# An attention and feed-forward kernel: queries on a second queue, rotation quarters between maxima, and small weights loaded in the fourth group

## The reference

```
q, k, v = xn @ wq.T, xn @ wk.T, xn @ wv.T        # 16 heads of 64
q, k = rope(q), rope(k)                          # x1*c - x2*s, x1*s + x2*c
scores = (q @ k.T) * 64**-0.5, causal
out = softmax(scores) @ v
x = x + layernorm(out @ wo.T)
x = x + layernorm(ffn(layernorm(x)))             # swiglu, mixture of 8 experts, swiglu
```

## Time and profile before

| | |
|---|---|
| median of 3 runs | 1265.85 us (1264.65 to 1266.01) |
| the profiled execution | 1265.46 us, its span 1263.7 us |
| PE busy | 1144.5 us, 91% of the span |
| DVE, ACT, POOL busy | 980.8, 958.8, 946.8 us |
| mean granted TensorE clock | 0.97 of full speed |
| first scores | at 62.09 us |

### The profile page before, as it was taken

The page is one execution under the profiler, slowest core; times in us unless marked ns, Lnnn a source line. Parts: engine busy times, 40 slices in busy tenths (PEclk is TensorE's granted clock), DMA queues, the critical chain, the costliest instruction groups (busy, mean ns, idle before and its releaser), DMA issues. The chain is left out here.

```text
span 1263.7 us, 34875 instructions
## 1 busy us (share of the span) xinstructions
PE 1144.5 (91%) x13531; PEld 789.1 (62%) x13531; DVE 980.8 (78%) x2230; ACT 958.8 (76%) x2199; POOL 946.8 (75%) x984
## 2 busy tenths in 40 slices
PE   4689999999989999999999999999999588999995
PEld 1246667676766676766767676767677355666562
DVE  7799777787968787878878787978575559767987
ACT  3668888878787878788787879787889665756574
POOL 3568889889898889898988889898767465334462
PEclk8699999999999999999999999999999798999996
DMA  6652425244251515252524425151601100000011
GB/s 200 146 134 65 115 59 134 61 109 102 67 135 35 135 35 136 56 124 59 135 63 108 106 63 131 39 135 35 152 19 47 51 1 2 1 1 2 1 34 34
DMA packets 50660, 97.03 MB, mean 77 GB/s; under 512 B 6720, under 2 KB 23360, under 8 KB 48448
## 3 DMA queue, kind: packets, MB, share of 16 engines
q1 hardware_dynamic: 50496, 94.81, 30.0%
HBM read 58.47 MB, written 34.60 MB: 74 GB/s over the span
## 5 line engine op out<-in xcount | busy, mean ns | idle before, releaser
L795 POOL TENSOR_TENSOR Plo<-P,Phi 128x512 f16<-128x512 f32 (+3 forms) x640 | 538.7, 868 | 128.5 <-ACT P L486 127.9
L483 ACT ACTIVATE Phi<-psS 128x512 f16<-128x512 f32 (+3 forms) x768 | 383.7, 500 | 148.9 <-PE psS L341 105.1
L486 ACT ACTIVATE P<-psS 128x512 f32<-128x512 f32 (+3 forms) x640 | 306.3, 479 | 0.0
L335 PE MATMUL psS<-Q,K 128*128 128x512 f16 (+3 forms) x768 | 251.5, 327 | 41.1 <-DVE Plo L642 37.1
L362 PE MATMUL psO<-V,Plo 128*128 128x65 f16 x2304 | 288.3, 194 | 0.0
L358 PE MATMUL psO<-V,Phi 128*128 128x65 f16 x2304 | 287.0, 192 | 0.0
L360 PE MATMUL psO<-V,Phi 128*128 128x64 f16 x2304 | 286.1, 191 | 0.0
L691 DVE TENSOR_REDUCE pmax<-psX 128x1 f32<-128x512 f32 x384 | 252.4, 683 | 23.6 <-PE psX L422 15.0
L358 PEld LDWEIGHTS psO<-V,Phi 128*128 128x128 f16 x2304 | 219.5, 98 | 56.6 <-issue 0.3
L338 PE MATMUL psS<-Q,K 65*128 65x512 f16 (+3 forms) x768 | 251.7, 328 | 0.0
L422 PE MATMUL psX<-K,Q 128*128 128x512 f16 (+4 forms) x768 | 226.5, 330 | 12.0 <-DMA Q<-HL 3.1
(11 more groups left out here) (197 smaller groups left out, 2165.0 us busy)
## 6 DMA issues: line engine op xcount, KB each, us to landing
K<-k_way SPq DMA_DIRECT2D x48, 512.0 KB, 7.1
k_way<-HL SPq DMA_DIRECT2D x64, 256.0 KB, 3.9
q_way<-HL SPq DMA_DIRECT2D x60, 256.0 KB, 3.8
Q<-q_way SPq DMA_DIRECT2D x60, 256.0 KB, 6.9
Q<-q_way SPq DMA_DIRECT2D x15, 512.0 KB, 11.7
out<-y SPq DMA_DIRECT2D x8, 256.0 KB, 2.2
y<-in_x SPq DMA_DIRECT2D x3, 512.0 KB, 10.9
hn<-in_x SPq DMA_DIRECT2D x3, 512.0 KB, 5.7
```

What stands on the lines that cost most here:

```text
L335: nc.tensor.matmul(out, M.K1[:, p, h, j * P:(j + 1) * P], M.Q1[:, p, h, c:c + w], start=True, stop=False)
L483: nc.scalar.activation(M.Phi[:, U % NP_, 0:w], X, ACT.Exp, scale=SCALE)
L486: nc.scalar.activation(full, X, ACT.Exp, scale=SCALE).then_inc(S.exp_done, 1)
L795: nc.gpsimd.tensor_tensor(M.Plo[:, U % NP_, 0:w], M.P32[:, U % NP_, 0:w], M.Phi[:, U % NP_, 0:w], ALU.subtract).then_inc(S.lo_pool, 1)
```

## The change

Five edits:
- `weights_later`: the thirteen small weight transfers move from SP's queue in the opening to the fourth group (slot 3), between the sending of its queries and the wait for its row of maxima.
- `first_query`: the four Q1 transfers of heads 0 and 1 are issued from ACT's queue, right behind the fourth rotated quarter's cast; those of heads 2 and 3 stay on SP's.
- First keys: each head's keys are loaded by a transfer of its own, as soon as that head's have arrived in DRAM, and TensorE waits head by head.
- The order of side items in slot -1: the second key quarter, both query quarters and the first two V pairs stand later, between and behind maxima; `X_SQUARE` places the batches of squares one by one.
- In the joins of maxima the copy is written as a maximum over one element.

```diff
-QK_EARLY = ((2, 3, 4, 5, 6, 7, 8, 9), (0, 1, 2, 3, 16, 17, 18, 19))
-V_FIRST = ((-1, 4), (-1, 5), (0, 1), (0, 3))
+QK_EARLY = ((2, 3, 4, 5, 6, 7, 8, 9), (0, 1, 16, 17, 25, 26, 29, 30))
+V_FIRST = ((-1, 24), (-1, 27), (0, 1), (0, 3))
...
-X_SQUARE = {(-1, 5): (1, 2), (-1, 17): (3,)}
+X_SQUARE = {(-1, 5): (1,), (-1, 17): (2,), (-1, 18): (3,)}
...
+W_SLOT = 3
...
+    def first_query(eng, queue, h):
+
+        rows = slice(h * HALF, (h + 1) * HALF)
+        for k in range(2):
+            queue.dma_start(M.Q1[k * HALF:(k + 1) * HALF, 0, h, :], M.HL[rows, 1, k, :]).then_inc(S.first_q[h], 16)
...
-                    if k == 0 and h % 2 == 0:
+                    if k == 0 and (s < 0 or h % 2 == 0):
                         if s < 0:
-                            pe.wait_ge(S.first_k, 32)
-                            pe.wait_ge(S.first_q[h // 2], 16 * GH)
+                            pe.wait_ge(S.first_k[h], 16)
+                            pe.wait_ge(S.first_q[h], 32)
...
                     rope_hi(item)
+                    if (s, *item[2:4]) == (-2, 1, 1):
+                        act.wait_ge(S.rope_hi, 4)
+                        for h in range(2):
+                            first_query(act, nc.scalar, h)
...
-                nc.vector.tensor_copy(M.pmax[:, 1, h, 0:5:4], M.pmix[:, h, 0:2, 3]).then_inc(S.max_parts, 1)
+                nc.vector.tensor_reduce(M.pmax[:, 1, h, 0:5:4], M.pmix[:, h, 0:2, 3:4], AX.X, ALU.max).then_inc(S.max_parts, 1)
...
-                                 M.HL[h * HALF:(h + 1) * HALF, 0, :, :]).then_inc(S.first_out, 16)
-                sp.wait_ge(S.first_out, 16 * GH)
-                for i in range(2):
-                    sp.dma_start(M.K1[:, 0, 2 * i:2 * i + 2], krows[:, 2 * i:2 * i + 2]).then_inc(S.first_k, 16)
+                                 M.HL[h * HALF:(h + 1) * HALF, 0, :, :]).then_inc(S.first_out[h], 16)
+                for h in range(GH):
+                    sp.wait_ge(S.first_out[h], 16)
+                    sp.dma_start(M.K1[:, 0, h], krows[:, h]).then_inc(S.first_k[h], 16)
...
-            for k, name in enumerate(("lin0_w", "swi1_w1", "swi1_w2", "lin1_w", "swi2_w1", "swi2_w2")):
-                sp.dma_start(M.wd[:, k, :], I[name]).then_inc(S.w_in, 16)
...
+                if s == W_SLOT:
+                    weights_later()
                 taken(sp, (s, "mt"))
```

## The result

The changed kernel takes 1280.62 us (median of 4 runs, 1280.06 to 1280.89) where the one before takes 1265.93 (4 runs, 1264.65 to 1266.33): ratio 1.0116 [1.0103, 1.0128], slower by 14.7 us. Its profiled span is 1278.9 us, 15.2 over the span before. The sign and both losses were as forecast; the size was not: it lies 1.6 us above the end of the range, and one step of the mechanism, the early landing of the queries, did not happen.

The account below looks back on a forecast made before the run. TensorE was taken as the bound in steady groups. Opening +4.3, fourth-group wait +3.6, lower clock +1.5 and later copies -0.5 made +8.9 us, 1274.7 on the median 1265.85, stated as 1274.5; range 1267 to 1279.

Parts of the forecast that it names:

- Queries and keys sooner: Opening: queries issued from ACT land early, so the first maximum starts at 36.5, 5.5 us sooner (bounds 35.6 to 39.8).
- T': Start of the opening's first maximum in the changed kernel, forecast at 36.5 us, bounds 35.6 and 39.8.
- Rival C: Opening: queries still land behind the keys, only 0.9 us of earlier issue is won; first maximum 41.1, total 1279; 6%.
- T: Start of the opening's first maximum in the kernel before, 42.01 us, after 3.09 us of waiting for a query transfer.
- V2: Third V pair on DVE in the opening, forecast at 72.0 instead of 66.29 us: +5.8.
- the opening's sum: Opening: +5.8 us at the third V pair less 1.5 for the long copy, +4.3 (bounds +3.4 to +7.6).
- the fourth group's two terms: Moved weights delay the row of maxima: TensorE waits 3.6 us (2.8 to 4.3), its lowered clock costs 1.5 (0 to 1.7).
- the chain from T': Opening: squares, V casts and query rotations following the first maximum put the first exponential at T'+33.2 = 69.7, 6.3 us later.
- V0: First V pair in the opening: ACT's cast stands behind all squares, done T'+18.3; DVE, there at T'+13.2, stands still 5.1 us.
- r6: First of two query rotation quarters of the second group, on DVE; forecast to end at T'+22.5, formerly T+10.8.
- POOL's chain behind r6: Opening: sums, casts, L816 and the table load up to the first exponential, 10.7 us in all, which nothing shortens.
- From there both orders are the same: Opening, behind the third V pair: old and new order run alike, so its +5.8 us shift passes on.

## Why the prediction was right and wrong

**What failed: "Queries and keys sooner".** I put T' at 36.5, "near the quick end, as only 128 KB of its own queue stand there". Measured: 41.23. The queries landed in 7.2 us at the least, slower than the 6.9 I had as the worst. Giving them another queue removed the keys of the same queue from ahead of them and nothing else; the 1.5 MB still shared the transfer engines. Rival C had this, at T' = 41.1 and 1279, and I gave it 6%. The Trainium skill ("DMA: Bandwidth & Descriptors", "Issuing engines are not separate DMA queues") says that all issuers share the same 16 engines; the traces agree: not more than the issue time was gained, T' is 0.8 us before T. The trace of before had spoken too: a later query transfer, issued when the keys had landed, took 2.7 us, those behind the keys 5.1 to 6.9. I read the difference as a place in a queue, without a row that said so. Holding back the bytes and not the queue brought 2.0 to 2.7 us. This one step is worth 4.7 us at T' and, with the roundings of the chain behind it, 4.9 at V2 (76.96 for 72.0); the opening's sum with it, +4.3 + 4.9, is the measured +9.2. With T' alone put right the forecast would have been 1279.2; the rest is the fourth group's two terms, below.

**What held: the chain from T'.** Measured against T', with the prediction in brackets: DVE's stop 5.10 us (5.1), V0 at +18.4 (wait ended where ACT was through with the squares, +18.3), r6 ended at +22.6 (+22.5), the first exponential at +33.4 (+33.2), V2 at +35.7 (+35.5). That ACT's squares ahead of V and the first maximum set the end was confirmed by moving each: squares behind V took 3.1 us off the wait and 5.3 off the lag (3.0 by the ratios), and a first maximum 7.1 us earlier moved the table by 7.2. That POOL's chain behind r6 does is read from the casts that wait for it (1.65 and 4.73 us); no run shortened it. That nothing later gives much back held: the lag stays within 2 us of its first value in every kernel that has the weights elsewhere. That DVE is the limit until 82 us did not hold in the changed kernel: behind V2 it waits four more times for TensorE and ACT (0.32, 0.59, 0.93 and 0.52 us).

**The copy, and some luck.** In the opening I took -1.5, and +10.7 at V2 became +9.2. But that is two errors that cancel. From V2 to the first steady row of maxima, the kernel before takes 62.3 us, with the maxima in place of the copies 59.1, the changed kernel 60.8, its order with the copies (the order alone) 63.7, and with the maxima and the weights back 61.1. So the long copy is worth 3.2 us in the old order and 2.6 in the new one, since it also brings on a stretch at a lower clock that I had not seen. In the order alone it stands at 91.28, TensorE's stop and the window behind it below:

```profile
91.28 1.67 DVE L714 COPY pmax<-pmix 128x2 f32<-128x2 f32 x1
```

```profile
93.81 0.23 PE L335 MATMUL psS<-Q,K 128*128 128x128 f16 x1 [2.05 <-DVE Plo L642]
```

```profile
96.00:98.00 2.00, 2.00 (x13) 0.90 (x12) 1.04 (x3) 0.00 (x0) 0.00 (x0) 0.54 0.10 26
```

In the changed kernel, without the copy, the clock there is 1.00:

```profile
78.00:80.00 2.00, 2.00 (x11) 1.03 (x10) 1.09 (x3) 0.00 (x0) 0.41 (x1) 0.50 0.97 245
...
90.00:92.00 2.00, 1.47 (x35) 1.24 (x33) 1.97 (x8) 1.36 (x6) 2.00 (x1) 1.00 1.05 244
```

What offsets it is some 1.7 us that the new order loses behind V2, and that the prediction, with "From there both orders are the same", put at nothing. The first of these two windows is the likely place, though no run isolates it: TensorE stands still for 3.50 us until DVE has done V2, and then works at 0.50 from 78 to 82.

Later I took -0.5 for a copy that the bounds gave up to 1.3; the lag falls by 1.0. That this is the copies' doing is not shown: with the weights alone and the order alone, which keep them, it falls by 0.8 and 1.2. In both, 0.6 of it falls in the ninth group, where the 1.47 us copy of the kernel before took 0.46, only by another timing. The steady copies of the weights alone:

```profile
L727 DVE COPY pmax<-pmix x15: 165/458/462, 126.1 to 944.6; 128x8 f32<-128x8 f32 x15
```

**The fourth group.** The place, the stop and the clock were as told; the sizes were low. I took 3.6 us of waiting (2.8 to 4.3): 5.17. The bounds priced the issues at the 6.2 to 7.7 us of the opening, but the first of them stand right behind q_way's 1 MB and cost more (8.6 us in all, the reading under "What I had not expected"). The clock: 1.5 taken, 2.0 measured. Together 5.1 taken, 7.1 measured in the lag, 5.8 and 6.2 by the ratios of two pairs of kernels. Removing the transfers from the opening of the kernel before gave 0, as priced.

**The sum.** +9.2, +7.1 and -1.0 make +15.3, the span's +15.2. Against the +8.9 of the prediction that is 6.4 too many (6.1 on the median): 4.9 from the queries, 2.0 from the fourth group, -0.5 from what comes back later.

## What to carry to other kernels

When a transfer is late, look for the bytes in flight when it is issued; here another issuing queue moved only the issue, while holding back bytes that nobody waited for yet moved the landing. Bulk issues belong in a stretch in which their queue is idle, never right ahead of a small row that the bounding engine waits for: the same thirteen issues cost 6 us in one place and nothing in the other, and they were free in the opening only as long as the first row of maxima came late. And before an item is moved ahead of another, look at what the third engine has in its queue at that point: here ACT's statistics stood ahead of a cast that DVE, and with it TensorE, needed.

## What I had not expected of the hardware

- The issue of a small transfer has no fixed price. Most took SP 0.43 to 0.48 us; the first ones behind the four q_way sends took 1.15, 1.60 for two and 1.97 for two, in both kernels that had them there to within 0.5 us. In the opening of the kernel before, behind the queries, the first pair took 2.37. Bytes in flight would explain it, but in the idle stretch one pair of the smallest ones took 2.76 us, so I leave the cause open.
- A float32 copy of two elements on DVE took 0.15 and 0.16 us or 0.89 and 1.67 us; the long ones end with a running POOL instruction. The same data written by a maximum over one element took 142 to 147 ns in all four places, and the steady ones 157 to 160 ns in all fifteen.
- That copy of 1.67 us cost twice its length: without it the row of maxima went out 3.1 us earlier, not 1.5. Behind it TensorE stood still for 2.04 us, up to 80.64, and worked at a granted clock of 0.65 from 82 to 84 and 0.50 from 84 to 86. In the new order the copy did the same: a stop of 2.05 us up to 93.81, then 0.60 and 0.54 from 94 to 98.
